# Rows of x gathered and searched for inside the loop; query and node state from two half-array products

## The reference

```python
h = x @ w_lin + b_lin
dense[dst, pos] = h[src]                 # n x 32 x 64; mask likewise
xb = mab(dense, dense, enc..., mask)     # self attention over a node's 32 slots
xp = relu(xb @ pma_lin_w + pma_lin_b)
p  = mab(seed, xp, pma..., mask)         # one seed query per node
dd = mab(p, p, dec...)
out = layernorm(x + relu(nan_to_num(dd)))
# mab(x, y): q, k, v = x@wq+bq, y@wk+bk, y@wv+bv; a = softmax(q k^T / 8, mask)
#            h = (a v) @ out_w + out_b + x;  return h + relu(h @ ff_w + ff_b)
```

## Time and profile before

| | us |
|---|---|
| median of 3 runs (4282.56 to 4283.9) | 4282.87 |
| the profiled execution | 4279.91 |
| its span | 4278.1 |
| mean granted TensorE clock | 0.955 |

### The profile page before, as it was taken

How to read it: one execution, slowest core, us unless ns; L and a number is a source line. 1 busy time by engine, 2 the same in 40 slices (tenths; PEclk the granted TensorE clock), 3 DMA queues, 4 the chain that set the end, 5 groups by cost and what they waited for, 6 DMA issues and landing times.

```text
span 4278.1 us, 111348 instructions
## 1 busy us (share of the span) xinstructions
PE 3488.9 (82%) x43804; PEld 2153.5 (50%) x43804; DVE 2677.3 (63%) x5467; ACT 1391.3 (33%) x2596; POOL 3155.2 (74%) x3353
## 2 busy tenths in 40 slices
PE   3716888888888888888888888888888888888887
PEld 1414555555555555555555555555555555555554
DVE  6744566666666666666666666666666666666665
ACT  0202333333333333333333333333333333333332
POOL 5777777777777777777777777777777777777771
PEclk9999999999999999999999999999999999999998
DMA  5633222222222222222222222222222222222230
GB/s 156 198 104 75 55 54 54 54 54 55 54 55 55 54 55 54 54 55 54 54 54 54 55 54 55 54 55 55 54 55 55 54 55 54 54 55 54 57 77 17
DMA packets 166583, 264.92 MB, mean 62 GB/s; under 512 B 95221, under 2 KB 109526, under 8 KB 166102
## 3 DMA queue, kind: packets, MB, share of 16 engines
q0 software_dynamic: 111328, 239.45, 21.0%
q1 hardware_dynamic: 54806, 18.27, 1.9%
HBM read 247.88 MB, written 11.23 MB: 61 GB/s over the span
## 4 chain that ended last, share of the span: by engine, by line
POOL 55%; issue 24%; PE 14%; DMA 5%; DVE 2%; POOLq 1%; ACT 0%; ACTq 0%; DVEq 0%
POOL gathered L578 52%; DMA gathered<-node_table,idx 3%; PE ps L688 3%; PE ps L651 3%; PE ps L669 2%; PE ps L704 2%; PE ps L723 1%; POOL xp_rows L544 1%; PE ps L753 1%; POOL gathered L544 1%; PE ps L727 1%; PE ps L763 1%; PE ps L745 1%; DVE hT L883 0%; POOLq L113 0%
## 5 line engine op out<-in xcount | busy, mean ns | idle before, releaser
L578 POOL DMA_INDIRECT gathered<-node_table,idx x3136 | 2966.1, 946 | 955.8 <-issue 939.0
L651 PE MATMUL ps<-ident,gathered 128*128 128x128 f32 x3136 | 526.1, 317 | 539.0 <-DMA gathered<-node_table,idx 538.4
L1071 DVE SCALAR_TENSOR_TENSOR xb<-ps,cols,h 128x512 f32<-128x512 f32 x392 | 294.3, 751 | 1020.4 <-PE ps L723 1020.2
L651 PEld LDWEIGHTS ps<-ident,gathered 128*128 128x128 f32 x3136 | 439.8, 211 | 633.5 <-issue 430.8
L772 ACT ACTIVATE xp_rows<-ps 128x512 f32<-128x512 f32 x392 | 234.1, 597 | 1184.2 <-PE ps L745 1184.2
L772 ACT ACTIVATE qT<-ps 128x512 f32<-128x512 f32 x392 | 234.1, 597 | 1052.3 <-PE ps L651 1052.3
L1126 DVE STREAM_TRANSPOSE probs_diag<-probs 32x512 f32<-32x512 f32 x784 | 550.9, 703 | 29.0
L669 PE MATMUL ps<-xb,pma_diag 128*128 128x512 f32 x784 | 478.6, 697 | 0.0
L688 PE MATMUL ps<-probs_diag,gathered 128*64 128x128 f32 x6272 | 454.9, 290 | 0.3 <-DVE h L993 0.3
L688 PEld LDWEIGHTS ps<-probs_diag,gathered 128*64 128x64 f32 x6272 | 359.1, 145 | 179.3 <-issue 169.5
L723 PE MATMUL ps<-h,ff_diag 128*128 128x512 f32 x784 | 440.7, 644 | 0.8 <-ACT xp L813 0.4
(11 more groups left out here) (184 smaller groups left out, 3324.2 us busy)
## 6 DMA issues: line engine op xcount, KB each, us to landing
gathered<-node_table,idx POOLq DMA_INDIRECT x3136
node_table<-hT SPq DMA_DIRECT2D x14, 448.0 KB, 4.4
qT<-in_x SPq DMA_DIRECT2D x13, 224.0 KB, 5.4
rows<-in_x SPq DMA_DIRECT2D x24, 112.0 KB
out_rows<-rows SPq DMA_DIRECT2D x20, 104.0 KB
gathered<-in_dst,win_idx POOLq DMA_INDIRECT x98, 4.2
xp_rows<-src_padded,sidx POOLq DMA_INDIRECT x98
src_padded<-in_src SPq DMA_DIRECT2D x1, 1562.5 KB, 15.9
```

The costliest lines, as they stand in the source:

```text
L578: pool.indirect_dma_start(out=gathered[:, s.slot(0, RING), t * ROW:(t + 1) * ROW], out_offset=None, in_=table, in_offset=bass.IndirectOffs ...
L651: mm = pe.transpose(ps[:, bank, p * P:(p + 1) * P], gathered[:, s.slot(0, RING), lo:lo + 2 * ROW - 1:2], ident[:, :])
L1071: V.scalar_tensor_tensor(xb[:, s.slot(L_FF, 2), :], ps[:, B_FF, :], c_("ff_b", P), h2[:, s.slot(L_FF, 2), :], ALU.add, ALU.max).then_inc(x ...
```

## The change

- **The gathered rows** are rows of x itself (64 numbers, 256 B); `node_table` and the stage that made it go. There are 391 octets, and the last gathers 5 tiles.
- **The search** moves into the loop. 1250 samples; `win_table` in DRAM holds for each sample 352 dst and 352 src entries side by side, written by four DMAs. One window gather per iteration on POOL (98 in all). `rows_of` (one count over 1250 columns) runs at the end of VectorE's steps that are 1 mod 4; `search` at the end of its steps that are 3 mod 4, for the iteration that begins five octets later: two counts over 352 columns, the number of edges, and nine predicated copies that shift the src window left by the bits of the start, each waiting for the one before, then a 32-column transpose into the indices. VectorE's index copy at the end of every step goes. The edge counts reach their layouts by two small products ahead of the scores of every other batch and two small VectorE instructions.
- **Query and state.** TensorE transposes x once (4 transposes, into B_Q), ScalarE copies it to `xT`, and after `pma` two products with K = 64 (rows 0 to 63 and rows 64 to 127 of `q_lin` and of `xT`) write 512 columns each, one to B_HX and one to B_Q; of each, one half of the partitions is the query, the other x @ w_lin. ScalarE evicts them in four copies of 64 partitions (`L_Q` = 1), ahead of hid, xp and avT in its queue. The score's right side is xT.
- Rows are laid out so that the output is stored by one DMA per part instead of four; weights are loaded from SP's and ScalarE's queues.

```diff
@@ search, VectorE
+            def rows_of(u, h):
+                V.tensor_scalar(flags[0][:, :], samples[:, :], node_f[:, bass.ds(u, 1)], None, ALU.is_lt, ALU.add,
+                                accum_out=win_row[:, h:h + 1]).then_inc(sampled, 1)
+                dve.wait_ge(sampled, u + 1)
+                V.tensor_scalar(win_idx[:, h:h + 1], win_row[:, h:h + 1], -1.0, None, ALU.add
+                                ).then_inc(win_idx_ready, 1)
+            def search(u, h, rounds):
+                dve.wait_ge(win_in[h], rounds * 16 + 16)
...
+                V.tensor_scalar(flags[1][:, :], dst_win, node, None, ALU.is_lt, ALU.add, accum_out=below[:, :]
+                                ).then_inc(found, 1)
+                V.tensor_scalar(flags[2][:, :], dst_win, node, None, ALU.is_le, ALU.add, accum_out=upto[:, :]
+                                ).then_inc(found, 1)
+                dve.wait_ge(found, u * 2 + 2)
+                V.tensor_copy(below_i[:, :], below[:, :]).then_inc(found_int, 1)
...
+                for b in reversed(range(BITS)):
+                    far = min((1 << b) - 1, WIN - (1 << b)) + DEG
+                    V.copy_predicated(src_win[:, 0:far], below_bits[:, b:b + 1].broadcast_to((P, far)),
+                                      src_win[:, 1 << b:(1 << b) + far]).then_inc(shifted, 1)
+                    wait_apart(dve, shifted, u * BITS + (BITS - b), dve_passed)
+                V.transpose(idx[:, h, :], src_win[:, 0:DEG]).then_inc(idx_ready, 1)
@@ end of VectorE's step
-                        V.tensor_copy(idx[:, s.slot(1, RING), :], idx_all[:, bass.ds(s.octet(1 - RING) * OCT, OCT)]
-                                      ).then_inc(idx_ready, 1)
+                if s.has_iteration(-5) and (s.looped or s.at >= 3):
+                    for lag in (3, 2, 1, 0):
+                        dve.wait_ge(g_in[s.slot(lag, RING)], s.round(lag) * (16 * OCT) + 16 * OCT)
+                    search(s.iteration(-5), s.slot(-5, RING) // OCTS_PER_IT, s.round(-5))
+                if s.has_iteration(-11) and (s.looped or s.at >= 1):
+                    rows_of(s.iteration(-11), s.slot(-11, RING) // OCTS_PER_IT)
@@ POOL's step
+                if s.has_iteration(-6) and (s.looped or s.at >= 2):
+                    u = s.iteration(-6)
+                    wait_apart(pool, idx_ready, u - 1, pool_passed)
+                    gather_windows(u, s.slot(-6, RING) // OCTS_PER_IT,
+                                   lambda sem_, count_: wait_apart(pool, sem_, count_, pool_passed))
@@ TensorE's step
-                    turn(s, 0, B_Q).then_inc(q_ps, 1)
...
-                    turn(s, 1, B_HX).then_inc(h_ps, 1)
+                    for p in range(PAIRS):
+                        mm = pe.transpose(ps[:, B_Q, p * P:(p + 1) * P],
+                                          gathered[:, s.slot(0, RING), p * P:(p + 1) * P], ident[:, :])
+                    mm.then_inc(x_ps, 1)
...
+                if s.has(L_Q):
+                    if s.has(L_BACK + 1):
+                        wait(pe, back_sb, s.octet(L_BACK))
+                    wait(pe, x_sb, s.octet(-1))
+                    for h, bank in ((0, B_HX), (1, B_Q)):
+                        hi = D * h
+                        pe.matmul(ps[:, bank, :], q_lin[hi:hi + D, :], xT[hi:hi + D, s.slot(L_Q, 4), :],
+                                  start=True, stop=True).then_inc(q_ps, 1)
@@ ScalarE's step
-                    copy(qT[:, s.slot(0, 4), :], ps[:, B_Q, :]).then_inc(q_sb, 1)
...
-                    copy(hT[:, s.slot(0, RING), :], ps[:, B_HX, :]).then_inc(h_sb, 1)
+                    copy(xT[:, s.slot(0, 4), :], ps[:, B_Q, :]).then_inc(x_sb, 1)
+                if s.has(L_Q):
+                    wait(act, s_ps, s.batch(L_Q + 4) + 1)
+                    wait(act, h2_sb, s.octet(L_Q + RING - 1))
+                    act.wait_ge(q_ps, s.octet(L_Q - 1) * 2)
+                    for h, bank in ((0, B_HX), (1, B_Q)):
+                        lo = D * h
+                        nc.scalar.activation(qT[lo:lo + D, s.slot(L_Q, 4), :], ps[lo:lo + D, bank, :], ACT.Identity,
+                                             bias=cols[lo:lo + D, col["q_b"]:col["q_b"] + 1]).then_inc(q_sb, 1)
+                    for h, bank in ((0, B_HX), (1, B_Q)):
+                        lo = D - D * h
+                        last = copy(hT[lo:lo + D, s.slot(L_Q, RING), :], ps[lo:lo + D, bank, :])
+                    last.then_inc(lin_sb, 1)
```

More of the change, by code:

```diff
@@ L44 @@
 EPS = 1e-5
-SAMPLES = 625
-HALF = 7
-CHUNK = 7
+SAMPLES = 1250
+SAMPLE_TILES = 10
+AHEAD = 2
+L_Q = 1
 L_SCORES = 2
@@ L124, in gnn_kernel, with tiles_of @@
     LAST = N - (ITS - 1) * P
[L125 to L129, removed]
+    OCTETS = -(-N // (QUADS * OCT))
+    STRIDE = E // SAMPLES
+    WIN = STRIDE + DEG
+    assert x.shape[1] == D and SAMPLES * STRIDE == E and STRIDE % DEG == 0 and WIN < 512 and ITS % 2 == 0
+    SAMPLE_ROWS = SAMPLES // SAMPLE_TILES
+    assert (SAMPLES - 1) // 16 * 16 == SAMPLES - 2
+    BITS = 9
+    def tiles_of(octet):
+        if not isinstance(octet, int):
+            return OCT
+        return min(max(-(-N // QUADS) - octet * OCT, 0), OCT)
     LOOP_FROM = L_Y + 1
@@ L245, in gnn_kernel @@
[L245 to L260, removed]
+        samples = sb("samples", [P, SAMPLES])
@@ new lines, in gnn_kernel @@
+        sample_i = sb("sample_i", [SAMPLE_ROWS, SAMPLE_TILES], I32)
+        sample_f = sb("sample_f", [SAMPLE_ROWS, SAMPLE_TILES])
+        sample_diag = sb("sample_diag", [SAMPLE_ROWS, SAMPLE_TILES, SAMPLE_ROWS])
+        ones = sb("ones", [SAMPLE_ROWS, P])
+        flags = [sb(f"flags{i}", [P, n]) for i, n in enumerate((SAMPLES, WIN, WIN))]
+        win_row = sb("win_row", [P, 2])
+        win_idx = sb("win_idx", [P, 2], I32)
+        windows = sb("windows", [P, 2, 2 * WIN + DEG], I32)
+        below = sb("below", [P, 1])
@@ L502, in _ @@
+            sp.dma_start(rows[0:LAST, ITS - 1, :], x[N - LAST:N, :]).then_inc(rows_in, 16)
             stores = 0
@@ L644, in _ @@
-            pe.matmul(ps[:, 2, 0:ITS], pool_perm, counts[:, :], start=True, stop=True).then_inc(permuted, 1)
-            pe.wait_ge(counts_read, 1)
-            def turn(s, c, bank):
-                for p in range(PAIRS):
-                    lo = 2 * p * ROW + c
-                    mm = pe.transpose(ps[:, bank, p * P:(p + 1) * P],
-                                      gathered[:, s.slot(0, RING), lo:lo + 2 * ROW - 1:2], ident[:, :])
-                return mm
             def step(s):
                 if s.has(0):
-                    wait(pe, q_sb, s.octet(0))
-                    pe.wait_ge(g_in[s.slot(0, RING)], s.round(0) * (16 * OCT) + 16 * OCT)
-                    turn(s, 0, B_Q).then_inc(q_ps, 1)
+                    wait(pe, x_sb, s.octet(0))
@@ L737, in step @@
                 if s.has(L_BACK):
-                    if s.has(0):
-                        wait(pe, h_sb, s.octet(-1))
+                    if s.has(L_Q):
+                        wait(pe, lin_sb, s.octet(L_Q - 1))
                     else:
@@ L905, in _ @@
+            for u in range(AHEAD):
+                rows_of(u, u)
             marked = [0]
@@ new lines, in _ @@
+            rows_of(AHEAD, 0)
+            dve.wait_ge(prep_pe, 10)
+            for i in range(2):
+                V.tensor_copy(wqT2[:, i, :], ps[0:D, 5, 0:D])
+                V.tensor_copy(wkT2_[:, i, :], ps[0:D, 5, D:2 * D])
+                last = V.tensor_copy(wvT2[:, i, :], ps[0:D, 5, 2 * D:3 * D])
+            mark(last)
+            search(1, 1, 0)
+            dve.wait_ge(prep_pe, 20)
+            V.tensor_tensor(c_("bo1", P), c_("b_lin", P), c_("bo1", P), ALU.add).then_inc(dve_chain, 1)
```

525 lines of the change are left out of this document (203 added, 322 removed).

## The result

The changed kernel takes 5471.39 us, median of 4 runs (5420.13 to 5522.07); the kernel before took 4283.39 us in the same job. The ratio is 1.273 [1.264, 1.283]: 27% slower. The prediction was 4823 us, 12.6% slower, with a range of 4450 to 5080. The direction was right; the size was short by more than half, and the time lies outside the range. The profiled execution took 5522.07 us for a span of 5520.1.

A forecast was written before the change was run, and what follows sets the result against it. POOL's gather issue bounds the kernel before; afterwards waits among TensorE, ScalarE and VectorE. First turn 62, 16 steps 165, 374 steps at 12.05 4507, end 84, around the span 5: 4823 us; range 4450 to 5080.

The forecast's parts named there:

- three places: TensorE's waits per four steps: hid in steps 1 and 2, xp in step 3, h in step 0; 47.0 us against POOL's 41.3.
- the search: VectorE's compares, nine shifts and transpose ahead of h of step 0: 6.5 us, between 4.3 and 8.6.
- the pair: TensorE's two q_lin products of 64 rows x 512 columns run side by side as one pass: 0.96 us.
- the rival of serial halves: q_lin's two products don't overlap: 0.86 us more in steps 1 to 3, 5066 us in all; chance 0.13.
- the clock: TensorE's lower clock level after gaps adds 1.2 us per four steps, 47.0 to 48.2; bounds 0 to 2.5.
- the long gap: TensorE idle 5.4 us once per four steps, in front of attend in step 0; 0.9 us added for the clock.
- the short ones: Two TensorE gaps of 2.6 us per four steps, in front of hid; 0.3 us added for the clock.
- the price of an eviction of 64 rows: ScalarE's four evictions of query and node state at 0.49 us each, done at 4.60 us into the step.
- The two count products: Two small TensorE products in step 2, put at 0.15 us together.
- the prediction's own 62 us: Time until the first octet's turn on TensorE, 62 us (45 to 80), taken as 235 us gained ahead of the loop.
- the tail: From the last octet's turn to the end: 78.75 us before the change, 84 after with one more light step.
- The rival on the other side: POOL's gather issue still sets the pace: 4166 us, if the search is shorter than some 1.7 us; chance 0.08.

The follow-up runs named there:

- the version of 4159 us: Changed kernel with hid and xp ahead of the evictions, avT between qT and hT, all nine search shifts in step 0 behind the diagonal's first half: 4159.29 us.

## Why the prediction was right or wrong

**Right: what bounds, and why.** That POOL would lose the pace, and to which three places. The places came out as forecast: hid behind four evictions, xp behind them in step 3, h behind the search. Every single removal gave time back.

**Right: the search.** Forecast 6.5 us; from the first compare (2039.31) to h (2045.66) it is 6.35. That it is so near is in part luck: the nine shifts with their waits took 3.60 us against 4.35, and the transpose with the way to h 0.57 against 0.2.

**Right: the pair.** 1.06 us, one pass; the rival of serial halves is out. The Trainium skill, "TensorE: Matmul & The Clock Gate", Part 3, states that distinct row groups run concurrently; this trace agrees, with 1.06 us for the pair where one 512-column product takes 0.96, and with starts less than 0.01 us apart.

**Wrong, the largest step: the clock.** The prediction added 0.9 us for the long gap and 0.3 for the short ones, 1.2 per turn, with 2.5 as the upper bound. In the turn shown, start to start and against the same products at full speed (0.96 for a 512-column product, 1.02 for attend, 0.54 for the counts in the run with the gaps filled), step 1 loses 0.69 + 0.89 (feed-forward, vo), step 2 0.40 + 0.88 + 0.41 + 0.91 + 0.89 (two small products, attend, counts, feed-forward, vo) and 0.1 in a small one behind them, step 0 0.63 in feed-forward and 0.14 in the scores: 5.9 us. Attend in step 0 is slow too (1.97), but the scores behind it wait for probs anyway. The runs agree in size: the gaps filled gave back 504 us, 5.4 per turn. The step that failed read its row too narrowly: the earlier trace rows prices the transposes directly behind a gap, and the sum took that as the whole loss. Here the lower level holds through five groups of products behind one gap. And the bulk was put on the wrong gaps: filling the two of 3.1 us gives back 444 of the 504 us.

**Wrong: the price of an eviction of 64 rows.** 0.49 each was taken from back-to-back copies of 128 rows. Measured: qT, which carries a bias here, 0.65 apart; hT 0.60; 2.50 us for the four, not 1.96. Fewer rows made none of them shorter. With hid seen 5.66 us into the step in place of 5.09, 0.57 in each of steps 1 to 3: 1.7 per turn.

**Wrong, small.** The two count products 0.54 at full speed, not 0.15. The loop's edge, 1.37 every second turn, was in no row that the sum used. Against this, in the step 0 behind it h came 5.60 us after the first transpose, not 7.27, mostly since that transpose was late itself while VectorE's search ran on, and the scores began 1.5 us earlier than forecast. The step took 14.83, not 15.55.

**Wrong: the row for the first turn of the kernel before.** The earlier trace rows gives 296.75 us as the first octet's transposes; it is the second's. The first octet's stand one row ahead:

```profile
286.70 1.95 PE L651 MATMUL ps<-ident,gathered 128*128 128x128 f32 x8 [16.22 <-DMA gathered<-node_table,idx]
```

So by the prediction's own 62 us the stage that goes was worth 225 us, not 235; with the measured 43.9 it gave 243. The forecast of the time doesn't use this row.

**The sum.** In the turn shown, 12.51 + 16.81 + 10.68 + 14.83 = 54.8 us against 48.2. By the terms: clock 4.7, evictions 1.7, counts 0.4, edge 1.4, less 1.5 for the earlier h: 54.9. This turn is somewhat shorter than the average. Over the 374 steps of the profiled execution (209.84 to 5429.12, below) a turn takes 55.8 us on average, since a step 0 that doesn't follow the edge takes 17.7 us against 15.1: TensorE waits 4.7 us in place of 3.7 for h and stops for another 1.0 at the scores. So the edge delays the transposes, but what stands behind it waits for the search in any case. The profiled execution then adds up: 4823, and 712 more in the 374 steps, 1 in the 16 before them and 7 in the tail (91.0 us from the last octet's turn, not 84), less 18 at the head (43.9, not 62) and 3 that this one execution doesn't have: 5522.

```profile
43.91 1.09 PE L552 MATMUL ps<-ident,gathered 128*128 128x128 f32 x4 [5.48 <-DMA gathered<-in_x,idx]
...
209.84 0.66 PE L552 MATMUL ps<-ident,gathered 128*128 128x128 f32 x4
...
5429.12 0.66 PE L552 MATMUL ps<-ident,gathered 128*128 128x128 f32 x4
```

**The range** took the clock's bounds, 0 to 2.5 us, as worked out from one row, and these were its error: with 5.9 the prediction's own sum would have given about 5270, and with the evictions 5430.

**The rival on the other side** was priced right (4166; 4159 measured, in another order) and judged right as not happening in this one. It named a search under 1.7 us as the point from which it decides. The runs show another: where in its queue the search stands. At its full length TensorE hardly waits for it once its compares fill VectorE's idle time ahead of xb in step 3 and its shifts stand behind h and probs.

## What to carry to other kernels

When work is added to an engine that is idle most of the time, look at what stands behind it in that engine's queue and put the result that another engine is waiting for first: here moves alone, with no instruction removed, took the time from 5457 to 4159 us. Price a new gap in TensorE's work by all the products that run at the lower level behind it, not by the gap and the first product alone: here gaps of 3.1 us, and in one run of 1.7 us, had such products behind them, and filling the two short gaps gave back far more (444 us) than filling the long one after them (60). Look at more than one turn: here a step 0 away from the loop's edge took 2.6 us longer than one behind it. After each removed wait read the waits again, for the next one takes over part of the gain.

## What the runs showed of the hardware that was not expected

- Work that nobody reads, put into TensorE's gaps, made the kernel 504 us faster (granted clock 0.80 to 0.98, the upper of the two levels, 2.4 GHz, nearly throughout).
- The same gap does not always cost the same. With two evictions both steps have a gap of 1.69 us in front of hid: in step 1 attend behind it takes 1.09 and feed-forward 1.12, in step 2 1.98 and 1.92. With the search split, gaps of 3.08 in both, in the turn shown: 1.09 and 1.12 behind the first, 1.22 and 2.07 behind the second. In the changed kernel the gap of 3.08 in step 1 leaves feed-forward at 1.86. So the length of the gap alone does not decide; whether it is what TensorE did before the gap, or something else, was not separated and stays open.
- Inside a series of score products TensorE sometimes stops for up to 2.2 us with nothing to wait for that the profile shows (62 times, 104.0 us, in the version of 4159 us); with half as many passes of the loop, 56.1 us in 38. In the changed kernel they stand almost only in the step 0 that doesn't follow the loop's edge. What they are was not tried.
- VectorE can idle about 5 us at the loop's edge, 3.3 to 3.5 ahead of h and 1.6 behind it, with the search split after three shifts (43 edges, 212 us; 217 with ScalarE's order changed too), and not at all with every shift behind the diagonal. The profile shows nothing that it waits for, and the cause is open.
